# Four-layer graph network on one core: in the edge stage, VectorE adds the gathered rows to the products and makes four one-hots in one instruction

## The reference, cut to what matters

```python
h = relu(layernorm(x))
msg_in = concat([h[src], h[dst], edge_attr_2], axis=-1)      # 128 + 128 + 2 columns
msgs = relu(msg_in @ mW1 + mb1) @ mW2 + mb2
agg = segment_sum(msgs, dst) / max(count(dst), 1)
x = x + layernorm(mlp(concat([h, agg])) + h) * gamma + beta
...
# layer 4 starts from h[src] + edge_attr_128, summed over dst
```

## Time and profile before

| | before |
|---|---|
| time, median of 3 runs (lowest to highest) | 5462.62 us (5461.38 to 5464.68) |
| profiled execution: its own time | 5468.74 us |
| its span from first to last instruction | 5466.9 us |
| busy: PE, DVE, POOL, ACT | 4884.9, 3182.8, 2124.8, 1810.1 us |
| mean granted TensorE clock | 0.974 of full speed |

### The profile page before, as it was taken

One profiled execution on the slowest core, in us unless ns is written; L12 is line 12 of the kernel. 1 busy time (PEld: TensorE's weight loads), 2 busy tenths in 40 slices (PEclk: granted clock), 3 DMA queues, 4 the chain that ended last, 5 costly groups with the idle time before them and its releaser, 6 DMA issues.

```text
span 5466.9 us, 122253 instructions
## 1 busy us (share of the span) xinstructions
PE 4884.9 (89%) x39674; PEld 4147.5 (76%) x39674; DVE 3182.8 (58%) x9488; ACT 1810.1 (33%) x3932; POOL 2124.8 (39%) x2627
## 2 busy tenths in 40 slices
PE   1899999998888888888888888889999999999998
PEld 1799999998777777777777777789997666666665
DVE  7899999996555555555555555641113444444444
ACT  2565665655111111111111111330003444444445
POOL 7311111111777777777777777600001111111000
PEclk8999999999999999999999999999999999999999
DMA  6344444444555555455555555247775554554554
GB/s 180 146 212 211 200 200 200 211 211 170 135 132 135 133 135 134 133 135 134 133 134 134 133 135 134 61 188 296 291 296 218 184 184 176 186 188 177 188 186 155
DMA packets 464827, 946.27 MB, mean 173 GB/s; under 512 B 107346, under 2 KB 395970, under 8 KB 426898
## 3 DMA queue, kind: packets, MB, share of 16 engines
q1 hardware_dynamic: 187778, 696.55, 34.0%
q0 software_dynamic: 58304, 121.69, 9.1%
q10 hardware_dynamic: 218448, 124.48, 8.4%
HBM read 691.90 MB, written 250.56 MB: 172 GB/s over the span
## 4 chain that ended last, share of the span: by engine, by line
PE 57%; POOL 20%; issue 12%; DVE 6%; DMA 3%; ACT 1%; ACTq 0%; DVEq 0%; POOLq 0%; SPq 0%
PE ps L1339 21%; POOL BIG L739 18%; PE ps L1146 10%; PE ps L1124 8%; PE ps L1108 4%; PE ps L1110 4%; PE ps L1224 3%; PE ps L1234 3%; DMA BIG<-table,IDX 2%; PE ps L1222 2%; DVE T L1603 2%; DVE BIG L1603 1%; POOL ACC L670 1%; PE ps L1317 1%; PE ps L1329 1%
## 5 line engine op out<-in xcount | busy, mean ns | idle before, releaser
L739 POOL DMA_INDIRECT BIG<-table,IDX x1664 | 1610.4, 968 | 537.6 <-issue 485.3
L1709 DVE TENSOR_TENSOR ACC<-ACC,ps 128x257 f32 x1664 | 702.9, 422 | 737.4 <-PE ps L1234 706.2
L1222 PE MATMUL ps<-T,BIG 128*128 x3328 | 694.5, 291 | 348.1 <-DMA BIG<-table,IDX 209.7
L1222 PEld LDWEIGHTS ps<-T,BIG 128*128 128x128 f32 x3328 | 527.5, 197 | 478.1 <-issue 472.0
L1234 PE MATMUL ps<-BIG 128*128 128x257 f32 x3328 | 806.5, 385 | 0.0
L1224 PE MATMUL ps<-BIG,ident 128*128 128x128 f32 x3328 | 761.2, 312 | 0.0
L1124 PE MATMUL ps<-H,ACC 128*128 128x128 f32 x4802 | 689.9, 284 | 0.0
L903 ACT ACTIVATE IDX<-SRC 128x4 int32<-128x4 uint16 x416 | 85.1, 205 | 1822.7 <-PE ps L1224 1732.1
L1234 PEld LDWEIGHTS ps<-BIG 128*128 128x128 f32 x3328 | 612.8, 194 | 73.5 <-DVE ACC L1709 0.3
L1124 PEld LDWEIGHTS ps<-H,ACC 128*128 128x128 f32 x4802 | 588.0, 191 | 0.2 <-ACT ACC L875 0.2
L875 ACT ACTIVATE BIG<-ps 128x392 bf16<-128x392 f32 x784 | 390.3, 498 | 467.7 <-PE ps L1110 467.7
(11 more groups left out here) (264 smaller groups left out, 7535.2 us busy)
## 6 DMA issues: line engine op xcount, KB each, us to landing
weight_mat<-ACC SPq DMA_DIRECT2D x49, 3136.0 KB, 9.2
BIG<-weight_mat SPq DMA_DIRECT2D x49, 3136.0 KB, 10.2
REL_WT<-count_mat SPq DMA_DIRECT2D x73, 1568.0 KB, 6.5
BIG<-count_mat SPq DMA_DIRECT2D x72, 1568.0 KB, 6.6
count_mat<-BIG SPq DMA_DIRECT2D x49, 1568.0 KB, 12.8
BIG<-rel_tab ACTq DMA_DIRECT2D x416, 128.0 KB, 3.3
BIG<-in_edge_attr SPq DMA_DIRECT2D x832, 64.0 KB
BIG<-in_edge_attr ACTq DMA_DIRECT2D x832, 64.0 KB
```

Of the source, the lines that this page charges most:

```text
L739: pool.indirect_dma_start(G[:, q * QUAD + u, :], None, tables[1], bass.IndirectOffsetOnAxis(ap=IDX[:, q, u:u + 1], axis=0)).then_inc(gathe ...
L1222: pe.matmul(to, DT[:, q % 2, u * P:(u + 1) * P], T1[:, b[q * QUAD + u], :], start=True, stop=False)
L1709: dve.tensor_tensor(to, to, PS[4 + u][:, 0:2 * F + 1], ALU.add).then_inc(slots_free, 1)
```

## The change

PE no longer multiplies the gathered rows by the identity and no longer waits for them. The two products that are left end in PSUM. A new DVE instruction (`rows_plus`) waits for the gathered rows and for the products, adds the two and writes the 512 columns of a quad into `HE`. ScalarE applies relu in place there. The four one-hot instructions of a quad become one tensor_tensor (`quad_onehots`) that compares `iota`, repeated four times, with the four columns of `REL`, each repeated 128 times. In `dve_quad`, one-hots and sums no longer alternate: the order is `DT` of quad n, rows of quad n-1, one-hots of quad n, then the four sums of quad n-2. The indices of a later quad are laid out once `rows_added` says that the rows have been read.

```diff
             def act_quad(i, q, more):
 
-                act.wait_ge(pre_ps, i * QUADS + (q + 1))
+                act.wait_ge(rows_added, i * QUADS + (q + 1))
                 if more:
                     stage(i * U + (q + QUADS) * QUAD, q)
-                act.wait_ge(slots_free, i * U + (q + 1) * QUAD)
-                act.activation(HE[:, q * QUAD:(q + 1) * QUAD, 0:F], PS[q % 2][:, :].rearrange("p (u f) -> p u f", f=F), ACT.Relu).then_inc(relu_done, 1)
+                hidden = HE[:, q * QUAD:(q + 1) * QUAD, 0:F]
+                act.activation(hidden, hidden, ACT.Relu).then_inc(relu_done, 1)
...
                     pe.wait_ge(a18_in[q], (i + 1) * 16)
-                    pe.wait_ge(gathered[q], (i + 1) * 16 * QUAD)
                     if on(2):
 
-                        pe.wait_ge(relu_done, i * QUADS + (q - 1))
+                        pe.wait_ge(rows_added, i * QUADS + (q - 1))
                     for u in range(QUAD):
                         to = PS[q % 2][:, u * F:(u + 1) * F]
                         pe.matmul(to, DT[:, q % 2, u * P:(u + 1) * P], T1[:, b[q * QUAD + u], :], start=True, stop=False)
-                        pe.matmul(to, A18[:, q, u * P:(u + 1) * P], w18[:, :], start=False, stop=False)
-                        mm = pe.matmul(to, ident[:, :], G[:, q * QUAD + u, :], start=False, stop=True)
+                        mm = pe.matmul(to, A18[:, q, u * P:(u + 1) * P], w18[:, :], start=False, stop=True)
...
+            def quad_first(i, q, second, third):
+
+                dve.wait_ge(relb_in[q], (i + 1) * 16)
+                if third:
+                    dve.wait_ge(pre_ps, i * QUADS + (q - 1))
+                dve.tensor_scalar(DT[:, q % 2, :], RELB[:, q, :], svec[:, 0:1], None, ALU.is_equal).then_inc(dt_ready, 1)
+
+            def rows_plus(i, q):
+
+                k = q % QUADS
+                dve.wait_ge(gathered[k], (i + q // QUADS + 1) * 16 * QUAD)
+                dve.wait_ge(pre_ps, i * QUADS + (q + 1))
+                dve.tensor_tensor(HE[:, k * QUAD:(k + 1) * QUAD, 0:F], PS[q % 2][:, :].rearrange("p (u f) -> p u f", f=F), G[:, k * QUAD:(k + 1) * QUAD, :],
+                                  ALU.add).then_inc(rows_added, 1)
+
+            def quad_onehots(i, q):
+
+                rel = REL[:, bass.ds(i * U + q * QUAD, QUAD)].rearrange("p (u a) -> p u a", a=1).broadcast_to([P, QUAD, P])
+                dve.tensor_tensor(D_[:, q * QUAD * P:(q + 1) * QUAD * P].rearrange("p (u d) -> p u d", d=P),
+                                  iota[:, :].rearrange("p (a d) -> p a d", a=1).broadcast_to([P, QUAD, P]), rel, ALU.is_equal).then_inc(onehot_ready, 1)
...
             def dve_quad(i, q, b, on):
 
-                def step_onehot(u):
-                    if on(0):
-                        last = dve.tensor_scalar(D[q * QUAD + u], iota[:, :], REL[:, bass.ds(i * U + q * QUAD + u, 1)], None, ALU.is_equal)
...
+                if on(0):
+                    quad_first(i, q, on(1), on(2))
+                if on(1):
+                    rows_plus(i, q - 1)
+                if on(0):
+                    quad_onehots(i, q)
+                if on(2):
+                    for u in range(QUAD):
+                        sum_waits(i * U + ((q - 2) * QUAD + u))
                         to = ACC[:, b[q * QUAD + u], :]
-                        dve.wait_ge(sum_ready, i * U + ((q - 2) * QUAD + u + 1))
-                        dve.wait_ge(slots_free, i * U + ((q - 2) * QUAD + u + U))
                         dve.tensor_tensor(to, to, PS[4 + u][:, 0:2 * F + 1], ALU.add).then_inc(slots_free, 1)
```

More of the change, by code:

```diff
@@ L292, in build_gnn @@
         a18_in = [sem(f"attr2_quad_in{k}") for k in range(QUADS)]
-        hid_ready, relu_done = sem("edge_hidden_ready"), sem("edge_relu_done")
+        rows_added, relu_done = sem("gathered_rows_added"), sem("edge_relu_done")
         stats_done, aggr_done, std_ready, norm_ready = sem("stats_done"), sem("aggr_done"), sem("std_ready"), sem("norm_ready")
@@ L1694, in _ @@
             dve.wait_ge(at_out, 16 * PARTS)
-            def dve_quad(i, q, b, on):
-                def step_onehot(u):
-                    if on(0):
-                        last = dve.tensor_scalar(D[q * QUAD + u], iota[:, :], REL[:, bass.ds(i * U + q * QUAD + u, 1)], None, ALU.is_equal)
[L1701 to L1705, removed]
+            def quad_first(i, q, second, third):
[3 more added lines that the diff above has]
+                dve.tensor_scalar(DT[:, q % 2, :], RELB[:, q, :], svec[:, 0:1], None, ALU.is_equal).then_inc(dt_ready, 1)
@@ new lines, in sum_waits @@
+            def sum_waits(step):
+                dve.wait_ge(sum_ready, step + 1)
+                dve.wait_ge(slots_free, step + U)
+            def dve_quad(i, q, b, on):
+                if on(0):
[7 more added lines that the diff above has]
+                        sum_waits(i * U + ((q - 2) * QUAD + u))
```

## The result

| | before | changed |
|---|---|---|
| median of the runs | 5463.45 us (4 runs, 5461.38 to 5464.68) | 5501.31 us (4 runs, 5496.09 to 5504.65) |
| ratio, 95% interval | | 1.0069 (1.0051 to 1.0086) |
| profiled execution, own time; span | 5468.74; 5466.9 us | 5496.09; 5494.3 us |
| line 739: busy, mean, maximum | 1610.4 us, 968 ns, 1221 ns | 1645.7 us, 989 ns, 1487 ns |
| line 739: first to last start | 2116.8 us | 2151.7 us |

The change costs 0.69%. The prediction was 5499 us, 0.66% slower. Both profiled executions lie at an edge of their kernel's times: that of the kernel before took 5468.74 us, more than any of the four runs, and that of the changed kernel was the fastest of its four. So the profiles differ by 27.4 us and the medians by 37.9.

The account below looks back on a forecast made before the run. POOL's gathers on line 739 were taken to pace the edge stage. +43 - 3 - 4 = +36 us on the profiled 5468.7 us gave 5505 us, less 6.1 us for the median: 5499 us, range 5476 to 5526 us.

Parts of the forecast that it names:

- The bound: Edge stage: POOL's gathers on line 739 set the pace, 1.273 us each, so work taken from PE gives nothing.
- The one-hots: +43 us: Large tensor_tensor one-hots in the edge stage delay POOL's gathers on line 739: 43 us, bounds 25 and 68 us.
- The stretch: Part of a DVE one-hot instruction in which a starting gather must wait: 0.475 us, from 0.085 us after its start.
- The small one-hots: -3 us: Removing the four small one-hots of a quad removes their delay of POOL's gathers: minus 3 us.
- DT: 0 us, within 5: DVE's DT instruction, unchanged but at another place in the order: 0 us, within 5 either way.
- The end: -4 us: After the last gather, the products lie before the landing, so 9.6 us becomes 5.7 us: minus 4 us.
- The sum: All terms, on the path: +43 - 3 - 4 = +36 us, giving 5499 us, +0.66%.
- PE's busy time: Sign: in the edge stage PE's busy time drops by about a quarter.
- rival 4: PE becomes the bound through its clock; at 1.2 GHz throughout the stage +330 us, 5790 us; chance 0.04.
- the large one-hots don't hold POOL: Rival: the new one-hots in the edge stage cost POOL nothing; -7 us, 5456 us; chance 0.08.
- Locked phases: Rival at line 739: one-hots lock clear of POOL's starts, 5442 us, chance 0.03; on the wrong side 5660 us, 0.02.
- The halved rate: Rival: the repeated operand halves DVE's rate, one-hots take 1.22 us; 163 us, 5620 us; chance 0.03.

Follow-up runs that it names:

- e9: The changed kernel run again, unedited, beside the kernel before on one chip; 5501.94 us, ratio 1.0067 to the kernel before.
- e1: The changed kernel with a quad's one-hots made again by four tensor_scalar instructions of 128 columns, rows_plus and new order kept; 5460.7 us, ratio 0.9995.
- e2: The kernel before with only the one-hots changed, to one tensor_tensor for four steps behind DT; 5519.16 us, ratio 1.0106.
- e3: The changed kernel with the one-hot tensor_tensor reading its column numbers from a PSUM copy, only REL from SBUF; 5459.48 us, ratio 0.9993.
- e4: The changed kernel with a quad's one-hots in two tensor_tensor instructions of 256 columns; 5484.99 us, ratio 1.004.
- e5: The changed kernel with column numbers in PSUM and DT a tensor_tensor reading its row number from PSUM; 6109.97 us on a slower chip, ratio 1.0215.
- e7: The same kernel as e5, run again where the kernel before took 5463.26 us; 5440.18 us, ratio 0.9957.

## Why the prediction was right

**The bound.** POOL's chain of gathers sets the length of the stage: idle time before line 739 is 537 to 538 us in each of the nine profiles of the table, and the spans differ by its busy time. The 466 us taken from PE bought nothing, as the prediction has it.

**The one-hots: +43 us.** Measured 34.7 us in the profile of the changed kernel and 38.7 us in e9's, inside the bounds of 25 and 68. That the cause is the two SBUF inputs was read from three gathers beside line 1538; e1, e2 and e3 show it from three sides. Two things within this term were off and cancelled in part. The stretch is longer: gathers that start 0.02 to 0.08 us behind the one-hots are held too, 0.53 us, and the maximum is 1487 ns, not 1.43 us. The lower edge of 0.085 us had been taken from DT, and for this instruction it is 0.02. The stretch is then 0.53 us, and even phases would give 416 x 0.53^2 / 2 / 1.273 = 46 us. But 176 of the 416 one-hots start 0.6 to 0.8 us before a gather, out of reach, and this took some 11 us off. That 43 us came within 8 us is therefore partly luck, since the phases (where the one-hots fall in POOL's period) were not known.

**The small one-hots: -3 us.** What the gathers inside sums and small one-hots carried before is 2.8 us, but only 1.0 us of it is the small one-hots' own, and 1.8 us is DT's at the second meeting place. The number is near; what stands behind it is two thirds another thing.

**DT: 0 us, within 5.** It went from 15.0 to 19.9 us: 171 of its 416 instances now start 0.2 to 0.3 us before a gather. That is at the end of the allowance. Its place in POOL's period moves it, as e1 (9.8 us) shows too.

**The end: -4 us.** 15.1 us became 11.1 us.

**The sum.** +36 us by the working. With the figures of the two profiles the terms would be 34.7 for the one-hots, 4.9 for DT, -2.8 and -4.0: 33 us. The one-hots were put 8 us too high and DT 5 us too low, so the sum is better than its terms, and part of that is luck. A term that nobody had: the median gather went from 958 to 955 ns, up to 5 us over 1664 gathers in the change's favour; why is open. In the profiled executions line 739's first to last start grew by 34.9 us and the end shrank by 4.0, the span grew by 27.4 us; the 3.5 us that are left over lie outside the stage. The medians differ by 37.9 us (interval 28 to 47). In e9 the stage, from first to last gather, takes 2155.3 us, 38.5 us more than before, and the one-hots carry 38.7 us.

**Where it was wrong.** PE's busy time was to fall by about a quarter. It fell from 1780 to 1663 us, by 7%: the products of line 1232 now count 447 ns each, not 385 as in the earlier trace rows. Those products wait for DVE's sum to free their bank (313 us of idle time before them), and the sums run one behind the other at 0.63 us (idle before line 1731, for itself: 125 us). That this wait also lengthens the products in the trace is my reading of it. Nothing hangs on it, but it was a wrong use of "busy". In rival 4 the working has a slip: at 1.2 GHz a quad would take PE 2 x 3.03 = 6.06 us against POOL's 5.09, so 0.97 x 416 = 403 us and not 330. The lower edge of the stretch and the second meeting place are named above.

**The rivals.** That the large one-hots don't hold POOL is refuted by e2. The Trainium skill's page "SBUF — State Buffer", section "Who interferes with whom", infers that tensor_tensor left the probe's transfers from GpSimd alone because making descriptors needs only the write interface; this does not carry over to the indexed gathers here (1.49 us in place of 0.95). The rule of the same section on two SBUF inputs fits them. Locked phases exist, mild in the changed kernel and strong in e2, on the costly side. The halved rate did not occur (683 ns). The granted clock in the stage was 0.95, where it had been 0.97; PE, busy for 77% of it, did not become the bound.

## What to carry to other kernels

When an engine that nobody seems to delay sets the pace, compare the mean and the median of its instructions: a tail in the durations was the work of another engine here, and the timeline told whose. Merging four short VectorE instructions into one long one makes a collision rarer but longer. In e4 the mean cost went roughly with the square of the held stretch. So a merge that saves VectorE time can cost the kernel. The phases matter as much: the same one-hots cost 35 to 39 us in the changed kernel and 56 in e2. If POOL's gathers are the bound, try to give VectorE's long instructions at most one tensor from SBUF and the other from PSUM. Making DT a tensor_tensor of that kind also freed POOL of it; its tensor_scalar form had held POOL with one large tensor and a column, both in SBUF. An operand that never changes can lie in a free PSUM bank, at the price of 0.2 us of VectorE time for DT.

## What the runs showed of the hardware that was not expected

- Against the tensor_tensor one-hots, a gather can lose only as it starts. POOL first by 0.01 us: gather 0.95 us, one-hots 0.72 us. Up to 0.02 us behind the one-hots the gather still goes first (0.95 us, and the one-hots take up to 0.75); from 0.03 us on it waits (1.48 us). Both outcomes occur at 0.02 us. For DT in the kernel before the edge lies between 0.08 us (gather undisturbed) and 0.09 us (gather 1.22 us).
- Against a tensor_scalar there is a second place. From 0.49 to 0.69 us behind a gather's start, DT takes up to 0.71 us in place of 0.48 and a small one-hot up to 0.52 in place of 0.28. Where DT starts just before that, 0.36 to 0.48 us, the gather takes up to 1.08 us.
- The hold ends 0.12 to 0.14 us before the end of the DVE instruction, for DT at 0.48 us, the halves of e4 at 0.42 us, the one-hots at 0.68 us and line 1538 at 1.89 us alike.
- One VectorE instruction of unchanged length in the trace (681 against 683 ns) costs the kernel 42 us or nothing, by whether its constant operand is read from SBUF or PSUM.
- The same program, the kernel before, took 5463 to 5464 us on three occasions and 5983 us on another chip. There the kernel of e5 and e7 was the slower by 2.2%, where elsewhere it is the faster by 0.4%.
